# Cross attention on one core: the next batch's units as two 64-row tiles of the array in one shared room, K split on GpSimd

## What is computed

```python
x = layer_norm(hidden_states, ln1_w, ln1_b)
q = (x @ q_w + q_b)            # k, v = ctx @ k_w + k_b, ctx @ v_w + v_b; split into 16 heads of 16
scores = jnp.einsum('bhqd,bhkd->bhqk', q, k) * scale
scores = jnp.where(mask, scores, mask_value)
out = jnp.einsum('bhqk,bhkd->bhqd', softmax(scores), v)
hidden = out @ cproj_w + cproj_b + hidden_states
y = gelu(layer_norm(hidden, ln2_w, ln2_b) @ fc_w + fc_b) @ proj_w + proj_b
return hidden + y
```

## Time and profile before

| what | value |
|---|---|
| median of 3 runs (range) | 739.46 us (738.22 to 741.74) |
| profiled execution: time | 738.16 us |
| profiled execution: span in the profile | 736.4 us |
| PE busy / ACT busy / DVE busy / POOL busy | 690.8 / 446.9 / 379.8 / 123.0 us |
| PE instructions (products) | 7026 |
| HBM read / written | 65.30 / 47.06 MB |

### The profile page before, as it was taken

One profiled execution on the slowest core, in us unless ns is written; L12 is line 12 of the kernel. 1 busy time (PEld: TensorE's weight loads), 2 busy tenths in 40 slices (PEclk: granted clock), 3 DMA queues, 4 the chain that ended last, 5 costly groups with the idle time before them and its releaser, 6 DMA issues.

```text
span 736.4 us, 16791 instructions
## 1 busy us (share of the span) xinstructions
PE 690.8 (94%) x7026; PEld 471.3 (64%) x7026; DVE 379.8 (52%) x848; ACT 446.9 (61%) x471; POOL 123.0 (17%) x90
## 2 busy tenths in 40 slices
PE   2579999999999999999999999999999988999997
PEld 2566665666566656665666566656665544697897
DVE  5755654554355435543555345534653372467663
ACT  5406668656865686668666765676567888622320
POOL 6222041003200320032002300230000071011010
PEclk9889999999999999999999999999999999999999
DMA  9678565446534653564456445645442700000001
GB/s 307 196 252 296 187 208 199 145 155 214 202 133 169 212 192 136 177 213 170 158 176 213 154 174 175 214 143 185 151 174 92 281 3 1 1 29 8 22 30 32
DMA packets 51082, 113.77 MB, mean 155 GB/s; under 512 B 6858, under 2 KB 39986, under 8 KB 49722
## 3 DMA queue, kind: packets, MB, share of 16 engines
q1 hardware_dynamic: 40488, 80.56, 32.5%
q10 hardware_dynamic: 10514, 32.08, 11.9%
HBM read 65.30 MB, written 47.06 MB: 153 GB/s over the span
## 4 chain that ended last, share of the span: by engine, by line
PE 77%; ACT 12%; DVE 5%; issue 2%; DMA 2%; ACTq 1%; DVEq 0%
PE O L1147 22%; PE S L1140 16%; ACT pr L596 12%; PE O L1077 11%; PE XB L1077 10%; PE O L1234 6%; PE S L1077 5%; PE XB L1114 2%; PE XB L1174 2%; PE MB L1127 2%; DMA k_scr<-kpart 1%; DVE kpart L741 1%; DVE kpart L744 1%; DVE g_lo L911 1%; DMA cols_s<-in_cols 1%
## 5 line engine op out<-in xcount | busy, mean ns | idle before, releaser
L596 ACT ACTIVATE pr<-S 128x1024 f32<-128x1024 f32 x416 | 400.5, 1024 | 204.2 <-PE S L1140 171.9
L1147 PE MATMUL O<-pr,vsl 128*17 128x256 f32 x3328 | 223.1, 382 | 1.3 <-DVE ot L806 1.3
L1140 PEld LDWEIGHTS S<-qst,kst 64*128 64x128 f32 x1664 | 115.0, 185 | 111.3 <-ACT pr L596 75.6
L1140 PE MATMUL S<-qst,kst 64*128 64x256 f32 x1664 | 169.6, 311 | 11.6 <-ACT pr L596 7.7
L1147 PEld LDWEIGHTS O<-pr,vsl 128*17 128x17 f32 x3328 | 74.7, 96 | 77.2 <-issue 14.9
L741 DVE TENSOR_SCALAR kpart<-O,cols_s 128x384 fp32r<-128x384 f32 x64 | 40.6, 634 | 117.2 <-PE O L1077 117.2
L528 POOL CAST c_hi<-cT 128x768 fp32r<-128x768 f32 (+1 forms) x28 | 23.9, 852 | 323.0 <-DMA cT<-in_ctx_t 170.4
L787 DVE TENSOR_REDUCE mx<-MB 128x2 fp32r<-128x512 f32 x64 | 44.1, 689 | 51.4 <-PE MB L1127 51.3
L1077 PE MATMUL O<-c_hi,w_hi 128*128 128x384 f32 (+1 forms) x128 | 52.3, 409 | 19.4 <-POOL c_lo L533 10.4
L755 DVE TENSOR_TENSOR vsl<-XB,rows_s 128x256 f32<-128x256 f32 (+1 forms) x104 | 43.3, 416 | 51.2 <-PE XB L1077 51.2
L1077 PE MATMUL XB<-w_hi,c_hi 128*128 128x256 f32 (+1 forms) x208 | 66.6, 320 | 2.9 <-DVE vsl L755 2.7
(11 more groups left out here) (96 smaller groups left out, 834.0 us busy)
## 6 DMA issues: line engine op xcount, KB each, us to landing
kst<-k_scr SPq DMA_DIRECT2D x89, 400.2 KB
k_scr<-kpart SPq DMA_DIRECT2D x48, 384.0 KB, 3.3
v_scr<-vsl ACTq DMA_DIRECT2D x8, 1768.0 KB, 6.0
cT<-in_ctx_t ACTq DMA_DIRECT2D x21, 384.0 KB, 4.7
k_scr<-kpart SPq DMA_DIRECT2D x16, 449.0 KB, 3.0
qst<-q_scr SPq DMA_DIRECT2D x87, 64.0 KB
q_scr<-qpart SPq DMA_DIRECT2D x16, 256.0 KB, 2.5
cT<-in_ctx_t ACTq DMA_DIRECT2D x7, 449.0 KB, 3.5
```

The costliest lines, as they stand in the source:

```text
L596: nc.scalar.activation(pr[:, n % PBUF, :], S[:, 2 * (n % 2):2 * (n % 2) + 2, :] .rearrange("p a n -> p (a n)"), ACT.Exp).then_inc(s_.exp_d ...
L1140: last = nc.tensor.matmul(S[:, 2 * (n % 2) + g_, j * LQ:(j + 1) * LQ], kst[rows_, s, j, kt * P:(kt + 1) * P], qst[rows_, s, j, :], start=T ...
L1147: last = nc.tensor.matmul(O[32 * h:32 * h + VW, 0, 0:LQ], vsl[:, par, s, kt, h * VW:(h + 1) * VW], pr[:, n % PBUF, h * LQ:(h + 1) * LQ], s ...
```

## The change

All units go through one room `U` of two banks; there is one pair of semaphores, `unit_ready` and `unit_taken`, and a unit waits until every unit before it is evacuated (`room_free`). In the head three rooms are used in turn, two of them in S. `KB`, `MB`, `XB` are gone.

Each 128-row product of a unit of a next batch becomes two products of 64 rows (`by_half`), one into each bank of the room, and VectorE adds the two sums. In the head key and value units stay 128 rows deep (batch 0), the x and query units are halves there too. Value units now hold two key tiles (7 units). The tables put K, V, maxima in other pairs, never two units in one pair. A key unit's sum is left whole in `kpart` by VectorE, and GpSimd writes its high and low part (`k_split`); SP stores it after that. The v bias is no longer added to V but, as a column, to the turned attention output (`bias_att`), since softmax weights sum to one. A maximum is reduced in one instruction over both banks. SP's order changes: the rows of slot 2 are issued behind the query's store, the last first-half key store and the fill of the next batch's slot 0. `store_v` moves from step 48 of the batch before to step 10.

```diff
-K_AT = {0: (0, 0), 2: (0, 1), 4: (0, 2), 6: (0, 3), 8: (1, 0), 10: (1, 1), 12: (1, 2), 14: (1, 3)}
-V_AT = {0: 0, 1: 1, 6: 2, 7: 3, 9: 4, 11: 5, 12: 6, 13: 7, 15: 8, 16: 9, 18: 10, 20: 11, 22: 12}
-MAX_AT = {3: (0, 2, 0), 5: (0, 2, 1), 9: (0, 3, 0), 11: (0, 3, 1),
-          15: (1, 0, 0), 17: (1, 0, 1), 21: (1, 1, 0), 23: (1, 1, 1)}
+K_AT = {0: (0, 0), 1: (0, 1), 2: (0, 2), 6: (0, 3), 9: (1, 0), 12: (1, 1), 14: (1, 2), 17: (1, 3)}
+V_AT = {13: 0, 18: 1, 19: 2, 22: 3, 23: 4, 24: 5, 25: 6}
+MAX_AT = {7: (0, 2, 0), 8: (0, 2, 1), 10: (0, 3, 0), 11: (0, 3, 1),
+          15: (1, 0, 0), 16: (1, 0, 1), 20: (1, 1, 0), 21: (1, 1, 1)}
-YN_AT, YT_AT = 13, 16
+YN_AT, YT_AT = 14, 17
...
+        def room(u):
+            if u < len(HEAD_UNITS):
+                return (S[:, 0:2, :], S[:, 2:4, :], U[:])[u % 3]
+            return U[:]
...
             for b in range(B):
                 first_fill(sp, b, 3)
                 if b + 1 < B:
-                    for c in range(3):
-                        store_k(b + 1, 0, c)
-                first_rows(b, 2)
-                if b + 1 < B:
+                    store_k(b + 1, 0, 0)
+                    store_k(b + 1, 0, 1)
+                    store_k(b + 1, 0, 2)
                     store_q(b + 1)
                     store_k(b + 1, 0, 3)
                     first_fill(sp, b + 1, 0)
+                first_rows(b, 2)
+                if b + 1 < B:
                     store_k(b + 1, 1, 0)
...
+            def k_split(b, mt, c):
...
+                pool.wait_ge(unit_taken, k_unit_no(b, mt, c) + 1)
+                nc.gpsimd.tensor_copy(high, total).then_inc(ks_done, 1)
+                pool.wait_ge(ks_done, u + 1 - UK)
+                nc.gpsimd.tensor_tensor(kpart[:, i, 1, 0:n], total, high.bitcast(F32), ALU.subtract).then_inc(kl_done, 1)
...
+                    nc.vector.tensor_scalar(total, halves[:, 0, 0:n], bk_s[:, mt:mt + 1], None, ALU.add).then_inc(k_half, 1)
+                    dve.wait_ge(k_half, u + 1 - UK)
+                    nc.vector.tensor_tensor(total, halves[:, 1, 0:n], total, ALU.add).then_inc(unit_taken, 1)
...
+                    nc.vector.tensor_copy(to, first_half).then_inc(v_half, 1)
+                    dve.wait_ge(v_half, KV * (b - 1) + i + 1)
+                    nc.vector.tensor_tensor(to, other, to, ALU.add).then_inc(unit_taken, 1)
...
+                nc.vector.tensor_reduce(mx[:, s % 2, :, j:HG:NJ].rearrange("p q g -> p g q"),
+                                        room(no).rearrange("p g (q k) -> p g q k", q=QT), AX.X, ALU.max,
+                                        negate=True).then_inc(unit_taken, 1)
...
+            def by_half(dst, w, m):
+
+                for i, (a, c) in enumerate(zip(w, m)):
+                    for g_ in range(2):
+                        rows_ = slice(g_ * HALF, g_ * HALF + HALF)
+                        last = nc.tensor.matmul(dst(g_), a[rows_], c[rows_], start=i == 0, stop=i == len(w) - 1)
+                return last
...
+            def room_free(no):
+
+                if no >= len(HEAD_UNITS):
+                    pe.wait_ge(unit_taken, no)
+                elif no >= 3:
+                    pe.wait_ge(unit_taken, no - 2)
```

More of the change, by code:

```diff
@@ L224, in build @@
         bq_s, bk_s, fcb_s = cols_s[:, 8:10], cols_s[:, 10:12], cols_s[:, 12:20]
-        bv_s, bc_s, pjb_s = (rows_s[:, i, :] for i in range(3))
+        bv_s = cols_s[:, 20:22]
+        bc_s, pjb_s = (rows_s[:, i, :] for i in range(2))
         mid = ExitStack()
@@ L554, in _ @@
                 x_bias(b)
+                for mt in range(2):
+                    for c in range(CH):
+                        k_split(b, mt, c)
             pool.wait_ge(mlpw_in, 32)
@@ L767, in q_evac @@
-            def q_evac(b, use):
+                dve.wait_ge(unit_ready, no + 1)
+                first_half, other = (room(no)[0:m, g_, 0:n * D].rearrange("p (t h d) -> p t h d", t=n, d=HD) for g_ in range(2))
+                to = vsl[0:m, b % 2, tiles, :].rearrange("p t (h w) -> p t h w", w=VW)[:, :, :, 0:HD]
+                if b == 0:
+                    nc.vector.tensor_copy(to, first_half).then_inc(unit_taken, 1)
+                else:
+                    nc.vector.tensor_copy(to, first_half).then_inc(v_half, 1)
+                    dve.wait_ge(v_half, KV * (b - 1) + i + 1)
+                    nc.vector.tensor_tensor(to, other, to, ALU.add).then_inc(unit_taken, 1)
@@ new lines, in xt_evac, with q_evac @@
+            def xt_evac(no):
+                dve.wait_ge(unit_ready, no + 1)
+                for k in range(KC):
+                    last = nc.vector.tensor_scalar(
+                        xT[:, k, :].rearrange("p (q g i) -> p g q i", q=QT, i=HALF),
+                        room(no)[:, :, k * P:(k + 1) * P].rearrange("p g (q i) -> p g q i", i=HALF),
+                        ln1_w[:, k:k + 1], ln1_b[:, k:k + 1], ALU.mult, ALU.add)
+                last.then_inc(unit_taken, 1)
+            def q_evac(b, no):
@@ L768, in q_evac @@
                 dve.wait_ge(some_in, 16)
-                dve.wait_ge(xb_ready, use + 1)
+                dve.wait_ge(unit_ready, no + 1)
+                halves = room(no)
                 for mt in range(2):
-                    last = nc.vector.tensor_scalar(qf[:, mt, :], XB[:, mt * LQ:(mt + 1) * LQ], bq_s[:, mt:mt + 1],
-                                                   some[:, b:b + 1], ALU.add, ALU.mult)
-                last.then_inc(xb_taken, 1)
+                    last = nc.vector.tensor_scalar(qf[:, mt, :], halves[:, 0, mt * LQ:(mt + 1) * LQ], bq_s[:, mt:mt + 1], None,
+                                                   ALU.add)
@@ L783, in max_evac @@
+            def max_evac(b, s, j, no):
                 dve.wait_ge(mx_zeroed, 1)
@@ L1118, in max_unit, with q_unit @@
-            def max_unit(b, s, j, kb, mb):
+                        for g_ in range(2):
+                            rows_ = slice(g_ * HALF, g_ * HALF + HALF)
+                            last = nc.tensor.transpose(room(no)[:, g_, k * P + q * HALF:k * P + (q + 1) * HALF],
+                                                       xn[rows_, q, k * P:(k + 1) * P], idn[rows_, rows_])
+                last.then_inc(unit_ready, 1)
+            def q_unit(no):
+                room_free(no)
+                for mt in range(2):
+                    last = by_half(lambda g_: room(no)[:, g_, mt * LQ:(mt + 1) * LQ],
+                                   [w_qc_s[:, 0, k, mt * P:(mt + 1) * P] for k in range(KC)], [xT[:, k, :] for k in range(KC)])
+                last.then_inc(unit_ready, 1)
```

383 lines of the change are left out of this document (183 added, 200 removed).

## The result

The changed kernel takes **742.88 us** (median of 16 executions, 739.24 to 745.73) against 739.48 for the kernel before on the same chip: ratio 1.0042, 95% interval 1.0027 to 1.0057. Forecast were 718.5 and a range of 702 to 735. The direction was wrong and the range did not hold the time. The loss is 0.4%, small but clear of the interval. The profiled execution took 742.1 with a span of 740.3.

A forecast was written before the change was run, and what follows sets the result against it. TensorE, busy 94%, was taken as the bound, ScalarE in pairs without a unit. Per batch -3.6 + 0.54 - 3.4 + 2.6 + 0.3 + 0.7 = -2.9, seven times -20, head -2, tail +1: -21, median 718.5 us, range 702 to 735.

The forecast's parts named there:

- Part 1: TensorE's unit products as 64-row halves: two take one wave, entries vanish, 3.6 us a batch saved, 0.54 lost.
- Part 3: One room for all units: each waits for the evacuation before it; new waits 2.6 us a batch, exponentials falling behind 0.3.
- rival (d): TensorE's half products do not overlap, a wave takes two: 21.7 us more a batch, 852 us; chance 0.02.
- the entry: On TensorE, a run of 128-row products costs 0.20 us extra: 0.09 before the first product, 0.10 before the second.
- Part 2: Existing waits in pairs without a unit (ScalarE) and units held by evacuation: all 3.4 us a batch go.
- the rows' 0.7: Scores of slot 2 wait at pair 13 for maxima rows queued on SP behind key store and fill: 0.7 us a batch.
- +0.54: Pairs 7 and 20, where a head group ends: a maximum is too short to cover VectorE's turn of O; loss 2 x 0.27.
- the walk: Batch followed pair by pair from unit start to free room: key units just fit (2.62 against 2.70), value units wait.
- Part 4: GpSimd splits K: 14 us a batch, hidden for itself; later key stores delay slot 2's rows, 0.7 us a batch.
- Rival (b): VectorE's evacuation is the bound: 17 units each wait 0.14 more, 2.4 us a batch, 735 us; chance 0.13.
- Head: Before the first exponential: key evacuations up to 5 us earlier, fills 2 later; taken as -2, bounds -5 and +2.
- Tail: End of the kernel: last projection changes mode twice (0.4), one more add before TensorE's wait (0.69): +1 us.

The follow-up runs named there:

- both whole: Changed kernel with key and value units 128 rows deep again in the shared room, without GpSimd's split of K; 743.11 us (1.0038 to the kernel before).
- three fixes: Changed kernel with inverse root in pair 21, fourth key unit before the query in the head, slot 2's rows before the fill; 734.67 us (0.9913).
- gates: Changed kernel with two GpSimd waits holding the split until VectorE is past divide and v bias; alone 735.25 us (0.9918), with the three fixes 726.79 (0.9818).
- control: Two changed kernels whose edits leave batches 2 to 6 alone: inverse root in pair 21 (738.42 us), key unit (0,3) before the query in the head (738.45).
- tiny split: Changed kernel with GpSimd splitting only 2 of the 384 or 449 columns of each key unit, all waits kept; 734.0 us (0.9933).
- head order: Changed kernel with key unit (0,3) before the query unit in the head, on TensorE and VectorE; 738.45 us (1.0).
- gates, root, head and rows mended: Changed kernel with the three fixes and the gates, 726.79 us (0.9818); with two head value units also ahead of the maxima, 725.34 (0.9785).

## Why the prediction was wrong, step by step

**Part 1, products: right, once Part 3's charge is put beside it.** The first and second product of a key unit behind scores were to be 0.17 apart. In pair 0 of batch 3 they are 0.18, in pair 1, whose unit follows another, 0.23:

```profile
285.29 0.35 PE L1096 MATMUL U<-c_hi,w_hi 64*128 64x384 f32 x2
285.47 0.34 PE L1096 MATMUL U<-c_lo,w_hi 64*128 64x384 f32 x2
...
288.00 0.42 PE L1096 MATMUL U<-c_hi,w_hi 64*128 64x384 f32 x2
288.23 0.36 PE L1096 MATMUL U<-c_lo,w_hi 64*128 64x384 f32 x2
```

Two halves of 384 columns take one wave, so rival (d) is out, and the entry of the earlier trace rows is gone. The full 0.20 comes in pairs 0, 9, 17 and 22 (2.91 to 2.71, 3.15 to 2.94, 3.08 to 2.89, 3.51 to 3.31). In 1 and 2 it is 0.12, in 18, 19 and 23 to 25 only 0.07. These are the pairs whose unit follows a unit, with little or no slack in the room, and there VectorE's two operations decide: the forecast for a value unit was 3.18 from start to free room, the pair takes 3.20. With whole units the pair takes 3.27. The prediction had 15 x 0.20 = 3.0 for key and value units and charged 5 x 0.22 = 1.1 of it back in Part 3 for the value units' second operation, net 1.9. Measured net: 1.9.

**Part 2 and the rest of Part 3: 1.0 too hopeful.** Forecast for all that is not half products of K and V, without the rows' 0.7: -0.6 for three other entries, +0.54, -3.4, 2.6 - 1.1 = +1.5, +0.3, so -1.7. Measured, before to both whole: -0.6, of which 0.1 is a wait for rows in one batch. The lengths that the walk gave for most pairs held within about 0.1: pair 7 2.52 (2.49), pair 8 2.06 (2.05), pair 10 1.98 (1.9), pair 16 2.71 (1.9 + 0.7), pair 19 3.20 (3.06 + 0.22). TensorE's wait for the reduce in pair 16 was there too (`U <- mx`, 0.5). Pair 16's wait was right in size by luck and only half right in cause: VectorE's divide and v bias stand before the reduce, but the pair is 2.42 with GpSimd's split out of the way, so 0.29 of the 0.7 is GpSimd's. Not foreseen were pairs 9, 11 and 22, 0.25 to 0.3 longer than the walk had them, with half products and with whole ones, together 0.8 a batch. Why was not tested.

**Part 4, "hidden for itself": the step that failed.** The work of GpSimd was costed by its own duration and by who waits for its result. Both were hidden, and GpSimd is busy only 27% of the span. What was not asked is what GpSimd's running does to the instructions beside it. The price: 1.2 us a batch (72.92 with the three fixes, 71.73 with the gates too: pair 3 0.90, pair 16 0.29), 7 us in six batches. Rival (b) had named "VectorE slowed beside a busier GpSimd" in half a sentence, but applied it to the adds that read PSUM, which kept their 0.62 and 0.56, and gave it no place; the place was the divide and the v bias between two evacuations. A sign was at hand: the divide's mean of 357 ns in the kernel before is 31 times 0.29 and once 2.40, and only the timeline shows such a spread.

The Trainium skill, "SBUF — State Buffer", section "Who interferes with whom", says that a VectorE instruction with two SBUF inputs contends with a GpSimd instruction that reads SBUF, that copies and `tensor_scalar` in their faster modes do so too, and that the one that issues second fully blocks until the other has ended. By that, this case's rows agree: 0.29 becomes 0.91 and 0.17 becomes 1.95, each ending with GpSimd's operation; the 0.17 at 133.28, which began before GpSimd's next, is not stretched; the turn of `att` with one input keeps 0.45. Had the rule been weighed, every VectorE operation with two inputs in SBUF, and the v bias, would have been charged up to the split's 0.87 wherever the walk put it beside one.

Part 4's rows of slot 2 were right in kind: 0.7 a batch charged, 0.47 measured in the changed kernel's execution and 0.1 to 0.2 in the two of the control.

**The first batch was not walked.** The tables are the same for it, but VectorE has the inverse root in pair 24 of batch 0 only. In the kernel before it had begun at 125.26, just behind GpSimd's last subtraction of the batch:

```profile
122.80 2.11 POOL L533 TENSOR_TENSOR c_lo<-cT,c_hi 128x900 fp32r<-128x900 f32 x1
```

Now it runs beside that subtraction, with the last value unit's evacuation queued behind it. Price: 5.5 us (pair 0 of batch 1 8.18 instead of 2.71; 4.6 to 4.7 in the executions of tiny split, head order and gates), of which TensorE's low level after the 3.08 of idle time is a part.

**Head: wrong sign.** That TensorE would run ahead of VectorE was right: the last key unit of the head is evacuated at 39.2 instead of 45.5:

```profile
38.53 0.69 DVE L737 SCALAR_TENSOR_TENSOR kpart<-S,cols_s,kpart 128x449 fp32r<-128x449 f32 x1
```

It brought nothing, because the chain had another limb. The text charged "2 later" for the constant rows and the query's store and weighed it against an earlier evacuation, as if terms of a sum. They are terms of a maximum: the first exponential waits for the later of two limbs, one through the last key store and one through the query's store, the first fill and the first row. By its own terms the head was up to +2, not -2. The first fill went out 3.6 later and the head measured +3.9, of which 2.7 goes with the order of two units. With that order mended the first fill leaves at 36.90, before the 37.09 of the kernel before, and the first exponential still starts 1.2 later than there: how much of this is the landing of DMAs is open. Tail: +0.3 for a forecast of +1.

**The sum.** Of the 25 us between the forecast span (715) and 740.3: head 6, batch 0 3.7, batch 1 6.6, batches 2 to 6 five times 2.0, tail -0.7. The 2.0 are 1.2 for GpSimd and 1.0 for pairs that the walk had too short, less 0.2 for rows that cost 0.5 and not 0.7. With gates, root, head and rows mended a middle batch is 71.73 and the time 725 to 727, 7 to 8 above the forecast and inside its range. That 71.73 is so near the 71.4 of the forecast is partly luck: the 0.7 for rows is mended away, so the walk itself is 1.0 short. The side effects, in GpSimd's timing, the first batch and the head, took more than the half products and tables gave.

**Left open:** the start of batch 0, where pair 1 takes 3.5 to 4.0 us in some executions and 5.6 to 5.9 in others, with no plain relation to the edit (in the changed kernel pairs 0 and 1 are 1.6 longer than in the kernel before and all other pairs together 0.8 shorter); the extra in pairs 9, 11 and 22; and whether a second room for units would do as well as the gates, which was not tried.

## What to carry to other kernels

When work moves to GpSimd, walk VectorE's order beside it and charge each VectorE operation of the kinds that were held up here (two inputs in SBUF, or a `tensor_scalar` from SBUF to SBUF) with GpSimd's remaining time, not only the work's own latency. When several resources are merged into one, a delay that reached nobody can become everybody's: look at each engine's odd jobs (a divide, an inverse root, a first batch) and not only at the steady rhythm. Where two limbs of a chain meet, take the later one; an earlier finish of the other is no term of the sum. And before a difference of a few tenths in a profile is given to an edit, look for a run whose edit does not touch that stretch.

## What the hardware showed that was not expected

- GpSimd beside VectorE: a multiply of 128 elements 0.29 us or 0.91, an add of a column to 256 elements 0.35 or 0.94, an operation on 12 elements 0.17, 0.93 or 1.95, each long one ending within 0.15 of the end of GpSimd's operation. The evacuations of `U` (one input in PSUM) were 0.62 and 0.56 with and without, the turn of `att` 0.45.
- An idle time of 3.08 us of TensorE is followed by 4.1 us at a granted clock of 0.50, with waves 0.32 apart for 384 columns, where they are 0.17 else; the pair with this wait of 3.1 us is 5.5 longer than the same pair of the later batches.
- One pair of steps that waits for row DMAs takes 2.77 in one batch and 3.66 in the next of the same execution, and another execution of the same stretch has 2.77 to 3.25.
- Two 64-row products of 384 columns with 128-column weight loads take one wave of 0.17.
